# A window-attention block on one core: the projection in four quadrants, fed by a re-sorting transfer, one period later

## What is computed

```
xn  = group_norm(x, 32 groups)                       # two channels per group
qkv = depthwise3x3(einsum('bchw,oc->bohw', xn, w_qkv) + b_qkv) + b_dw      # 192 channels
q, k, v = 8x8 windows of qkv                         # n windows, 4 heads, 16 channels, 64 pixels
attn = softmax(einsum('nhcx,nhdx->nhcd', q, k) * temperature)              # 16 x 16 per head
out  = einsum('nhcd,nhdx->nhcx', attn, v)
gate = gelu(einsum('nhcx,yx->nhcy', v, w_mlp) + b_mlp)
out  = x + einsum('bchw,oc->bohw', out * gate, w_proj) + b_proj
```

## Time and profile before

| | before |
|---|---|
| median of three runs | 679.36 us |
| the profiled execution, device time | 681.82 us |
| its span | 680.0 us |
| TensorE (PE) busy | 625.8 us, 92% |
| TensorE weight loads (PEld) busy | 549.1 us, 81% |
| VectorE (DVE) busy | 511.6 us, 75% |
| ScalarE (ACT) busy | 482.8 us, 71% |
| mean granted TensorE clock | 0.973 |
| transfers | 72.28 MB, mean 106 GB/s |

### The profile page before, as it was taken

How to read it: one execution, slowest core, us unless ns; L and a number is a source line. 1 busy time by engine, 2 the same in 40 slices (tenths; PEclk the granted TensorE clock), 3 DMA queues, 4 the chain that set the end, 5 groups by cost and what they waited for, 6 DMA issues and landing times.

```text
span 680.0 us, 32438 instructions
## 1 busy us (share of the span) xinstructions
PE 625.8 (92%) x15044; PEld 549.1 (81%) x15044; DVE 511.6 (75%) x790; ACT 482.8 (71%) x631; POOL 0.3 (0%) x5
## 2 busy tenths in 40 slices
PE   3788799999999999999999999999999999999954
PEld 2687698888989898888989898888989798888843
DVE  4872688887888888786878676786868676876684
ACT  3652678787877778786877778786877778786722
POOL 0000000000000000000000000000000000000000
PEclk9997899999999999999999999999999999999975
DMA  9872115335171714132050504132150504112022
GB/s 363 263 217 72 33 50 166 110 86 208 33 232 49 234 59 149 66 102 93 8 191 5 195 4 142 60 94 106 29 173 4 198 3 152 44 50 80 4 82 44
DMA packets 29240, 72.28 MB, mean 106 GB/s; under 512 B 9801, under 2 KB 16329, under 8 KB 24233
## 3 DMA queue, kind: packets, MB, share of 16 engines
q1 hardware_dynamic: 28674, 68.57, 31.0%
q10 hardware_dynamic: 432, 1.65, 0.7%
HBM read 53.44 MB, written 16.78 MB: 103 GB/s over the span
## 4 chain that ended last, share of the span: by engine, by line
PE 87%; ACT 5%; DVE 3%; issue 2%; DMA 1%; ACTq 0%; DVEq 0%
PE unit_ps L709 28%; PE unit_ps L674 26%; PE rest_ps L796 10%; PE rest_ps L787 6%; PE rest_ps L763 6%; PE rest_ps L747 6%; PE rest_ps L773 4%; ACT z L326 2%; DMA patches<-in_hot 1%; ACT dw L326 1%; PE rest_ps L643 1%; PE rest_ps L674 1%; PE unit_ps L636 0%; DVE scores L511 0%; DVE scores L536 0%
## 5 line engine op out<-in xcount | busy, mean ns | idle before, releaser
L326 ACT ACTIVATE z<-unit_ps 100x768 f32<-100x768 f32 x244 | 184.9, 808 | 60.1 <-PE unit_ps L674 60.1
L674 PE MATMUL unit_ps<-consts,patches 64*100 64x192 f32 x1984 | 195.0, 336 | 8.6 <-ACT z L326 6.6
L709 PE MATMUL unit_ps<-z,dw 103*64 103x64 f32 (+2 forms) x6144 | 194.3, 224 | 3.0 <-issue 1.7
L709 PEld LDWEIGHTS unit_ps<-z,dw 103*64 103x64 f32 (+2 forms) x6144 | 185.5, 139 | 10.7 <-issue 8.6
L674 PEld LDWEIGHTS unit_ps<-consts,patches 64*100 64x100 f32 x1984 | 153.6, 164 | 25.8 <-ACT z L326 11.2
L326 ACT ACTIVATE qkv<-unit_ps 128x1024 f32<-128x1024 f32 x78 | 79.1, 1014 | 31.5 <-PE unit_ps L709 31.4
L511 DVE TENSOR_TENSOR scores<-rest_ps,consts 128x512 f32<-128x512 f32 x64 | 44.1, 689 | 51.6 <-PE rest_ps L747 51.6
L503 DVE TENSOR_TENSOR gate<-rest_ps,gate 128x512 f32<-128x512 f32 x64 | 44.1, 689 | 47.5 <-PE rest_ps L787 44.6
L796 PE MATMUL rest_ps<-gate,consts 128*128 128x256 f32 x256 | 75.1, 417 | 1.1 <-DVE gate L503 1.0
L347 ACT ACTIVATE v_t<-rest_ps 128x512 f32<-128x512 f32 x64 | 38.2, 597 | 40.5 <-PE rest_ps L773 38.9
L341 ACT ACTIVATE scores<-scores 128x512 f32<-128x512 f32 x64 | 40.4, 631 | 33.2 <-DVE scores L518 31.6
(11 more groups left out here) (55 smaller groups left out, 530.5 us busy)
## 6 DMA issues: line engine op xcount, KB each, us to landing
staged<-in_x SPq DMA_DIRECT2D x17, 1024.0 KB, 4.9
out_y<-staged SPq DMA_DIRECT2D x15, 1024.0 KB, 5.4
T<-in_x SPq DMA_DIRECT2D x12, 1152.0 KB, 6.7
seen<-in_x SPq DMA_DIRECT2D x32, 256.0 KB, 2.9
qkv<-in_x SPq DMA_DIRECT2D x6, 1024.0 KB, 13.9
T<-in_x SPq DMA_DIRECT2D x3, 1088.0 KB, 6.7
staged<-in_x SPq DMA_DIRECT2D x2, 512.0 KB, 22.9
out_y<-staged SPq DMA_DIRECT2D x4, 256.0 KB, 3.0
```

The lines of the kernel that those rows point to most:

```text
L326: return nc.scalar.activation(to, of, ACT.Copy)
L674: last = nc.tensor.matmul(to[0:NPATCH, t, b * QKV:(b + 1) * QKV], patches[image, b, g], w1[image], start=True, stop=True)
L709: last = nc.tensor.matmul(to[h * HW:(h + 1) * HW, m // 8, m % 8 * NW:(m % 8 + 1) * NW], dw[0:used, c, :], z[0:used, c, :], start=True, sto ...
```

## The change

`project` now works in four quadrants of the array: four products of 64 x 64 by 256 columns, for image b and band half t. For that the 64 channels of one image must lie in 64 adjacent partitions, so the gated product is re-sorted by SyncE with eight transfers per step of 32 partitions x 1 KB each (`to_rows`, new tile `by_row`, two buffers). `project(i - 2)` stands in step i. `gate` gets a fourth buffer. `proj_ps` moves from a bank of its own to the upper halves of two banks, `turn_ps` to the lower halves. In steps 0 and 1 `turn_v` is eight ordinary products with 64 rows, 128 weight columns and 64 moving columns in place of four transposes. Units after `apply_probs` are gone: the next `score` stands directly behind it. The two gates of step 1 are spread over steps 0 and 1; in step 3 one of the two goes through `unit_ps` as a unit of its own. In the last chunk `project` writes to `unit_ps`, and the very last step still uses the 128-row form, `project_last`, whose weight is loaded late into `seen`.

```diff
-GATES = 3
+GATES = 4
 def gates_in(i):
-    return (0, 1) if i == 0 else (i + 1, i + 2) if i % 2 and i + 2 < STEPS else ()
+    n, a = i // BATCHES + 1, i % BATCHES
+    if a < 2:
+        return (i + 2,)
+    return (i + 1, i + 2) if a == 3 and n < CHUNKS else ()
+def ahead(i):
+    return 2 if i % BATCHES < 2 else 1
+def in_unit(j):
+    return j > 1 and j % BATCHES == 1
...
+            def to_rows(j):
+                sp.wait_ge(mixed_ready, j + 1)
+                if j > 1:
+                    sp.wait_ge(proj_done, j - 1)
+                for b in range(2):
+                    for h in range(2):
+                        for t in range(2):
+                            here, there = 2 * (h ^ b) + t, 2 * b + h
+                            sp.dma_start(by_row[there * BLOCK:(there + 1) * BLOCK, j % 2, t],
+                                         gate[here * BLOCK:(here + 1) * BLOCK, j % GATES, b].rearrange(
+                                             "p g y -> p (g y)")).then_inc(by_row_in[j % 2], 16)
...
+            for i in range(STEPS):
+                n, a = i // BATCHES, i % BATCHES
+                if i:
+                    to_rows(i - 1)
+                if a == 0 and n + 2 < CHUNKS:
                     load_t(n + 2)
-                if n:
+                if a == 2 and n:
                     store(n - 1)
-                load_seen(BATCHES * n + 1)
-                if n and n + 1 < CHUNKS:
+                if a == 3 and n and n + 1 < CHUNKS:
                     prefill(n + 1)
...
-            exp_table(0)
             for g in range(0, COLS, 2):
                 evacuate_first(act, copy, g)
-            for v in range(0, 6, 2):
-                evacuate_dw(act, copy, 0, v)
+            evacuate_dw(act, copy, 0, 0)
+            evacuate_dw(act, copy, 0, 2)
+            gelu(0)
+            gelu(1)
+            exp_table(0)
+            evacuate_dw(act, copy, 0, 4)
...
                 if a < 2:
+                    early = 1 if i and a == 0 else 2
+                    if i == 0 or not more:
+                        v_up(i)
                     if more:
-                        evacuate_mix(act, copy, n, 8 * a)
-                        evacuate_mix(act, copy, n, 8 * a + 1)
-                    exponent(i)
-                    v_up(i)
-                    if more:
-                        for g in range(8 * a + 2, 8 * a + 6):
-                            evacuate_mix(act, copy, n, g)
+                        for g in range(early):
+                            evacuate_mix(act, copy, n, 8 * a + g)
                     exponent(i)
                     if more:
+                        if i and a == 0:
+                            evacuate_mix(act, copy, n, 1)
+                            evacuate_mix(act, copy, n, 2)
+                        if i:
+                            v_up(i)
+                        for g in range(3 if i and a == 0 else 2, 6):
+                            evacuate_mix(act, copy, n, 8 * a + g)
...
                 dve.wait_ge(proj_done, i + 1)
+                if i + 2 < STEPS:
+                    dve.wait_ge(v_t_ready, i + 3)
...
-                if now:
-                    gate_up(now[0])
-                elif i:
-                    residual(i - 1)
+                for j in now:
+                    gate_up(j)
+                if n == CHUNKS:
+                    residual(i - 2)
                 divide(i)
                 turn(i)
-                if now:
-                    if i:
-                        residual(i - 1)
-                    gate_up(now[1])
+                if i > 1 and n < CHUNKS:
+                    residual(i - 2)
+                if i == STEPS - 1:
+                    residual(i - 1)
...
             def turn_v(i):
...
                 for g in range(BATCH):
+                    v = windows(i, g)[:, 2]
+                    if i % BATCHES < 2:
+                        for h in range(2):
+                            rows = slice(h * HW, (h + 1) * HW)
+                            last = nc.tensor.matmul(turn_ps[:, h, g * HW:(g + 1) * HW], v[rows], ident[rows, rows],
+                                                    start=True, stop=True)
+                    else:
+                        last = nc.tensor.transpose(turn_ps[:, g // 2, g % 2 * P:(g % 2 + 1) * P], v, ident)
...
             def project(i):
 
+                pe.wait_ge(by_row_in[i % 2], 128 * (i // 2 + 1))
+                if i < STEPS - BATCHES:
+                    pe.wait_ge(mixed_ready, i + 2)
+                if i:
+                    pe.wait_ge(out_ready, i)
+                for t in range(2):
+                    for b in range(2):
+                        rows = slice(b * HW, (b + 1) * HW)
+                        last = nc.tensor.matmul(projected(i)[t * C:(t + 1) * C, b, :], proj_row[rows],
+                                                by_row[rows, i % 2, t].rearrange("p (g r c) -> p r g c", r=WS, c=WS),
+                                                start=True, stop=True)
+                last.then_inc(proj_done, 1)
...
+            for v in range(3):
+                depthwise(0, v)
+            gates(0, 0)
+            gates(1, 0)
+            for v in range(3, 6):
                 depthwise(0, v)
             for i in range(STEPS):
+                now, units_now = gates_in(i), fillers(i)
+                if i == 0:
+                    turn_v(i)
+                    fill(units_now[:2])
                 if i % BATCHES == 0:
                     qkv_of(i // BATCHES)
                 score(i)
+                fill(units_now[2:4] if i == 0 else units_now[:ahead(i)])
+                for j in now:
+                    gates(j, i)
+                if i > 1:
+                    project(i - 2)
                 if i:
+                    turn_v(i)
+                fill(units_now[4 if i == 0 else ahead(i):])
+                if i == STEPS - 1:
                     project(i - 1)
                 apply_probs(i)
-                fill(units_now[cut[2]:])
-            project(STEPS - 1)
+            project_last(STEPS - 1)
```

139 lines of the change are left out of this document (78 added, 61 removed).

## The result

The change makes the kernel slower: 721.39 us median (714.09 to 723.57, 4 runs) against 679.2 (678.96 to 680.39) for the kernel before on the same chip, ratio 1.0599, 95% interval 1.0518 to 1.068. The prediction was 676, its range 653 to 694. The profiled execution took 719.44 (span 717.6) against 681.82 (span 680.0); all comparisons of traces are between spans. In the table further down two of the four executions of resort_behind and one of the six of resort_behind_old ran in a slower state of the core; their medians are over all executions, their ratios over the others.

A forecast was written before the change was run, and what follows sets the result against it. TensorE was taken to bound the kernel (87% of the chain). Ordinary groups -2.6, early groups +1.6, start -3.5 and end +0.9 us gave -3.6: from 679.36 to 676, range 653 to 694.

The forecast's parts named there:

- TensorE's prices: Predicted TensorE piece lengths: gates with projection 1.06 us, projection alone 0.55, turn by products 0.9 in steps 0 and 1.
- Rival 4: Projection: the quadrants don't overlap with 256 columns, +69 us, 748; chance 0.06 together with rival 3.
- Rival 2: Turn in steps 0 and 1: weight loads don't overlap, 1.5 us instead of 0.9, +18, 694; chance 0.18.
- The walk through the steps: Steps 0 to 3 of an ordinary group: +0.89, -0.48, -0.30, -0.37 us, together -0.26 a group.
- The transfers: Re-sorting on SyncE: eight issues of 0.27 us, landed at 6.4, 5.7 of slack before the projection; cost nothing.
- The start: First group: two gelus and their table loads leave step 0, gates move between depthwise units; together -3.5 us.
- The end: Last group, first score to last apply_probs: 28.9 us against 28.05, +0.9, including the last wait for a transfer.
- Rival 3: Projection waits for the late re-sorted product; 1 us late each step costs 60 us; chance 0.06 together with rival 4.
- Rival 1: TensorE's saving arrives whole: projection 0.42 us cheaper in 60 steps, -25, with the start 651; chance 0.15.

The follow-up runs named there:

- resort_behind: Kernel before plus eight unread re-sorting transfers per step, issued behind the step's large ones, with store and prefill late: 710.04 us, ratio 1.0354.
- resort_behind_old: Kernel before plus eight unread re-sorting transfers issued last in each step, all large transfers in their old places: 703.01 us, ratio 1.0349.
- no_resort: Changed kernel without the re-sorting transfers from step 2 on, later projections reading old data: 698.34 us, ratio 1.028 to the kernel before.
- turn_whole: no_resort with four whole transposes for the turn in steps 0 and 1 in place of eight products: 691.14 us, ratio 1.0176 to the kernel before.
- sp_order_later: before_sp_order with SyncE held in every step until VectorE's reciprocal, no small transfers: 701.4 us, ratio 1.0335 to the kernel before.
- early_gates: Kernel before with the first two gates and gelus among the first depthwise units and one table load less: 677.34 us, then 678.12 when repeated.
- tail_order: Changed kernel with, in the last group, the exponential ahead of the v copy and the residual behind VectorE's transpose: 717.49 us.
- before_sp_order: Kernel before with the changed kernel's SyncE order and four gate buffers, but no re-sorting transfers: 687.12 us, ratio 1.0124.
- before_late_store: Kernel before with only the 1 MB store and the prefill held back to later in the group: 687.91 us, ratio 1.0126.
- before_two_copies: Kernel before with the changed SyncE order, four gate buffers and two unread 128-partition transfers per step in place of eight: 703.55 us, ratio 1.035.
- behind_mended: Changed kernel with whole transposes, tail_order's last group, store and prefill a step earlier, small transfers behind the large ones: 757.08 us, ratio 1.1129 to the kernel before.

## Why the prediction was wrong

**TensorE's prices: right.** Gates with projection 1.06 (predicted 1.06), projection alone 0.59 (536.62 to 537.21; 0.55), turn by products 0.94 (0.9), turn in steps 2 and 3 0.59 (0.55). Rival 4 (quadrants that don't overlap, 748) is out. Rival 2's condition, 1.05 or more for the turn, isn't met. (Rival 4's 748 counts its 69 us from 679, rival 2's 694 counts its 18 from 676; from 676 rival 4 would be 745.)

**The walk through the steps: nearly right.** 10.20, 9.66, 8.26, 10.42 against 9.93, 9.43, 8.08, 10.3. A group gains nothing but loses 0.54 instead of winning 0.26. The run of six units has three stalls in step 0 (0.26, 0.29, 0.21) and takes 5.58 where I said 5.4; step 2 is 0.18 longer. Over 14 groups that is 0.8 x 14 = 11 us, and it is the smaller part. no_resort's shortest group has 10.20, 9.67, 8.26 and 10.06, together 38.19, so the order alone lost 0.19 a group, 0.45 more than I said. turn_whole shows that the turn, priced right at +0.37 in half of the steps, decides the sign (37.57 or 38.19).

**The transfers: the failed step.** I wrote that an issue costs 0.27, "2.2 to 2.5 us of SyncE", that the band load hardly touches the transfers, that everything behind the issues is "needed a step or more later", and "Cost nothing". The 0.27 came from a line of small DRAM loads; here it is 0.59 and up to 1.8, and the eight of a step take 4.9 to 6.9 us, 5.7 in the middle. The landing (2.0, I said 2.9) and the missing wait of project in the middle were right. What failed is the question I asked. I asked who needs the data of a late transfer; nobody does. I didn't ask what the transfer collides with when it runs elsewhere. TensorE takes 342 matmul instructions in the 10.67 us of step 3 and 136 in the 9.04 of step 0: 32 and 15 per us, each with its weight load. The kernel before has its large transfers in steps 0 and 1, where DMA share was 0.77 and 0.33, and almost none in steps 2 and 3 (0.02, 0.03). These numbers stood in my own rows, and I read only the lengths. The change moves store and prefill into steps 2 and 3, which my sum has no term for; late places for them cost 8.5 to 9.5 us in the kernel before. And it moves all large transfers some 5 to 9 us further on, which by itself costs 14.3 more there (sp_order_later). That the places decide is shown; that it is the number of instructions per us beside them is my reading of the counts, since no run changed that number alone.

The Trainium skill (Runtime: NRT & Kernel Launch, Instruction fetch mechanics) says that instructions come in blocks of 256 by a DMA queue of the engine's own, and that the cost of crossing a block is mostly hidden. The packets of 16.4 KB and the stops at every time the same number of 256 agree, and so does the kernel before, whose 102 packets in groups 1 to 14 leave no idle time (the 0.60 ahead of the first score of each group comes at any distance from a packet, 0.2 to 3.3 us). The stretches of up to 3.13 us in the kernel after, 20.2 us in all, don't: under other DMA traffic the cost isn't hidden here.

**The start: right for the middle, too small an effect to confirm.** I said -3.5; the profile has -6.1, but the start of kernels with an unchanged start lies anywhere from 105.8 to 109.6. early_gates, which does the main part alone, gives between -0.4% and +0.1% in time.

**The end: wrong, +0.9 against +10.2.** Some 5 us belong to the order of residual and v copy (tail_order, in the profiles). Of the transfer of step 62 I wrote 1 + 2.5 + 2.9 = 6.4; with issues of 0.6 its project waits 4.67, and no_resort, which has no such wait, ends in 41.9 in place of 46.5. The lower clock (0.57 for 0.72) I had not priced.

**The sum by runs.** Places of the large transfers 8.5 (before_sp_order); their delay 14.3 (sp_order_later less before_sp_order); the order with its end 11.2 (no_resort less before_sp_order), of which the turn is 7.2 (turn_whole); the last group's wait for transfers about 4.6 (profiles): 38.6 of the 42.2. The rest, 3.6, isn't resolved. The parts needn't add up so exactly: no_resort's large transfers don't stand where before_sp_order has them (table), and against before_late_store, which is nearer, the order would be 10.4. Nor is the 14.3 the delay's alone in the changed kernel: a delay without small transfers is enough for it, but before_two_copies and groups 5 to 14 of resort_behind lose as well with small transfers and hardly a delay.

**The rivals.** Rival 3 (project waits for the re-sorted product) is wrong for this kernel except for the last wait, and right for behind_mended. Rival 1 was half true: TensorE's work fell a little (busy 621.0 against 625.8), and the time didn't come with it. The rival that I lacked is what happened: large transfers that delay TensorE's instruction packets where it uses them up fastest.

## What to carry to other kernels

When a change adds issues to a queue or moves a transfer, ask not only who needs its data but what runs beside it: in the windows, set each stretch's DMA share beside its number of TensorE instructions, and keep the large transfers beside the pieces with few instructions. A queue's issues are work of its engine (here 0.6 us each, whatever the size), and they shift every large transfer behind them. Put small transfers behind the large ones only where the large ones stand beside few instructions and no load that waits for another engine stands between: with the statistics' load there, groups 1 to 4 lost 25 us. That load issued ahead of the step's small transfers and its wait was not tried.

## What the runs showed of the hardware

- TensorE gets its instructions in packets of 16.4 KB for 256 instructions, and stops where one packet's are used up if the next starts less than about 2.2 us ahead of that: 0.65 to 3.13 us at a time, always at the same number of 256 (all 13 stretches after, 140 of 141 in all traces). Here a packet usually starts some 225 instructions ahead, so about one packet is in hand. A store and a prefill of 1 MB each per group in the wrong place are enough (before_late_store, +9.5 us).
- A transfer between partitions holds SyncE for 0.59 us with 32 KB, 0.58 with 4 KB and 0.56 with 128 KB (before_two_copies); a three-row load from DRAM holds it for 0.27.
- Eight products with 128 weight columns and 64 moving columns take 0.94, four transposes of 128 by 128 0.58 in the same place. The products' row of weight loads is as long as they are (0.97 us for 16 loads from 517.23 on), which fits loads that set the time.
